# Reciprocals of the softmax denominators on a 128 by 8 tile, with a changed order of visits and four seeds on VectorE

## What is computed

```python
xn = _layernorm(x)
qkv = (xn @ W_qkv).reshape(b, s, 16, 64, 3)
q, k, v = qkv[..., 0], qkv[..., 1], qkv[..., 2]
weights = softmax(einsum('bqhd,bkhd->bhqk', q, k) / 8)
s = einsum('bhqk,bkhd->bqhd', weights, v).reshape(b, s, 1024) @ W_out
x = x + s * silu(mixture_of_experts(xn))
```

## Time and profile before

| | |
|---|---|
| median of 3 runs | 1840.99 us (1839.34 to 1845.72) |
| profiled execution, its own time | 1841.47 us |
| its span, first to last instruction | 1839.6 us |
| mean granted TensorE clock | 0.982 |
| busy: PE, DVE, ACT, POOL | 94%, 84%, 79%, 79% of the span |
| one pair in the middle of the loop | 42.1 us |

### The profile page before, as it was taken

One profiled execution on the slowest core, in us unless ns is written; L12 is line 12 of the kernel. 1 busy time (PEld: TensorE's weight loads), 2 busy tenths in 40 slices (PEclk: granted clock), 3 DMA queues, 4 the chain that ended last, 5 costly groups with the idle time before them and its releaser, 6 DMA issues. The chain is left out here.

```text
span 1839.6 us, 32373 instructions
## 1 busy us (share of the span) xinstructions
PE 1727.4 (94%) x9247; PEld 924.8 (50%) x9247; DVE 1547.9 (84%) x2180; ACT 1459.2 (79%) x1954; POOL 1444.4 (79%) x869
## 2 busy tenths in 40 slices
PE   5899999999999999999999999999999899975687
PEld 5444444444444444444444444444444677763456
DVE  7888888888888888888888888888888878888886
ACT  4488888888888888888888888888888777864553
POOL 5388888888888888888888888888888256654664
PEclk9899999999999999999999999999999999997899
DMA  7212121212212121212122121212122777331000
GB/s 258 79 36 80 36 80 46 80 46 69 78 52 86 34 80 36 80 46 80 46 69 82 51 83 34 80 36 80 46 80 62 241 218 218 115 99 48 0 18 29
DMA packets 125334, 143.31 MB, mean 78 GB/s; under 512 B 26737, under 2 KB 106673, under 8 KB 122098
## 3 DMA queue, kind: packets, MB, share of 16 engines
q1 hardware_dynamic: 120306, 132.61, 23.6%
q0 software_dynamic: 4992, 10.27, 1.7%
HBM read 87.20 MB, written 27.64 MB: 62 GB/s over the span
## 5 line engine op out<-in xcount | busy, mean ns | idle before, releaser
L1562 POOL TENSOR_TENSOR psum_k<-psum_k,probs 128x1024 f32<-128x1024 f32 x384 | 929.3, 2420 | 103.9 <-ACT probs L1499 83.8
L1499 ACT ACTIVATE probs<-ps_s 128x1024 f32<-128x1024 f32 x512 | 497.0, 1024 | 149.9 <-PE ps_s L1319 149.9
L1328 PE MATMUL ps_v<-probs,V 128*64 128x512 f32 x2056 | 497.8, 605 | 0.0
L1581 DVE TENSOR_REDUCE mxh<-ps_three 128x2 f32<-128x1024 f32 x264 | 318.5, 1207 | 98.3 <-PE ps_three L1286 98.2
L1483 ACT ACTIVATE ps_s<-peak 128x1024 f32<-128x1024 f32 x224 | 245.1, 1132 | 0.0
L1483 ACT ACTIVATE ps_s<-qkv_raw 128x1024 f32<-128x1024 f32 x224 | 245.0, 1131 | 0.0
L1622 DVE RECIPROCAL e_y_row<-e_y_row 128x128 f32<-128x128 f32 x256 | 241.0, 941 | 0.0
L1328 PEld LDWEIGHTS ps_v<-probs,V 128*64 128x64 f32 x2056 | 124.8, 136 | 228.6 <-issue 209.7
L1319 PE MATMUL ps_s<-e_ew 64*128 64x512 f32 x1536 | 199.0, 391 | 0.0
L1562 POOL TENSOR_TENSOR psum_k<-probs 128x1024 f32<-128x1024 f32 x64 | 152.8, 2388 | 47.2 <-ACT probs L1499 39.4
L854 POOL DMA_INDIRECT results<-e_y_row,e_y_at x92 | 102.6, 1115 | 82.0 <-ACT e_y_row L795 52.8
(11 more groups left out here) (320 smaller groups left out, 3184.4 us busy)
## 6 DMA issues: line engine op xcount, KB each, us to landing
e_ew<-w_split SPq DMA_DIRECT2D x23, 1024.0 KB
qkv_raw<-peaks SPq DMA_DIRECT2D x33, 512.0 KB, 3.9
V<-e_x_raw SPq DMA_DIRECT2D x33, 512.0 KB, 3.6
peak<-peaks SPq DMA_DIRECT2D x32, 512.0 KB, 4.3
xs_hi<-xh SPq DMA_DIRECT2D x16, 512.0 KB, 4.0
xs_lo<-xl SPq DMA_DIRECT2D x16, 512.0 KB, 5.0
rows<-in_blank_d SPq DMA_DIRECT2D x4, 1483.5 KB, 16.9
e_x_raw<-rows SPq DMA_DIRECT2D x23, 258.0 KB
```

Of the source, the lines that this page charges most:

```text
L1328: ins = nc.tensor.matmul(ps_v[rows, :], V[par][:, kt, rows], probs[:, t % RING, x, :], start=kt == 0, stop=kt == KT - 1)
L1499: nc.scalar.activation(probs[:, t % RING, :, :], ps_s[t % 2][:, :, :], ACT.Exp, scale=SCALE).then_inc(p_done, 1)
L1562: nc.gpsimd.tensor_tensor(acc, probs[:, (t - 1) % RING, :, :] if kt == 1 else acc, probs[:, t % RING, :, :], ALU.add).then_inc(add_done, 1)
L1581: nc.vector.tensor_reduce(mxh[:, kh, t, :], max_bank(unit, i)[:, :, :], AX.X, ALU.max).then_inc(m_done, 1)
```

## The change

It replaces the eight reciprocals of 128 x 128 words of a pair by two of 128 x 8. The denominators of a half are equal over the 64 rows of a head, so 2 x 512 of them are distinct. SP copies one row of each head (`den`) to 128 partitions of 8 words (`flatten`, two DMAs within SBUF), DVE inverts `flat_den` into `flat_inv`, SP writes it to a new DRAM tensor `shares` (`inverse_out`) and spreads it again over 64 rows for each head into `rden` (`inverse_back`, two DMAs). `half_pair` puts these five requests around the two of `spread`. The order of the visits changes, DVE writes the seeds of steps 3, 7, 11 and 15, and the experts' low part (`we_lo`) is made in an output visit. Both halves of a pair now have the same DVE order.

```diff
-    BY_V = (3, 13)
+    BY_V = (3, 7, 11, 15)
-    VISIT = [("K1",), ("Q0", "den1"), ("out0",), ("V0",), ("Q1", "den0"), ("out1",), ("V1",), ("K0",)]
+    VISIT = [("Q0", "den1"), ("out0",), ("K1",), ("V0",), ("Q1", "den0"), ("out1",), ("K0",), ("V1",)]
...
+            def spread_back(unit, hf):
                 sp.wait_ge(mx_out, unit * 16 + 16)
                 sp.dma_start(peak[hf][:, :, :].rearrange("p c x -> p (c x)"), g.peaks[hf:hf + 1, :].to_broadcast([P, 2 * CH])).then_inc(peak_in, 16)
+            def flatten(n, hf):
+                sp.wait_ge(xa_done, reads(n, f"den{hf}"))
+                for x in range(2):
+                    sp.dma_start(flat_den[x * DH:(x + 1) * DH, :], den[x * DH:x * DH + 1, :].rearrange("a (c k) -> a c k", c=DH)).then_inc(inv_moved, 16)
+            def inverse_out(k):
+                sp.wait_ge(inv_done, k + 1)
+                sp.dma_start(g.shares[:, :].rearrange("a (c k) -> (a c) k", c=DH), flat_inv[:, :]).then_inc(inv_moved, 16)
+            def inverse_back(k):
+                sp.wait_ge(inv_moved, inv_moved_out(k))
+                for x in range(2):
+                    sp.dma_start(rden[x * DH:(x + 1) * DH, :], g.shares[x:x + 1, :].to_broadcast([DH, CH])).then_inc(inv_moved, 16)
+            def half_pair(n, unit, hf):
+                k = n * 2 + 1 - hf
+                flatten(n, hf)
+                inverse_out(k)
+                spread(unit, hf)
+                inverse_back(k)
+                spread_back(unit, hf)
...
                 sp.dma_start(xs_hi[:, :].bitcast(F32), g.xh[:, batch].bitcast(F32)).then_inc(xs_in, 16)
                 sp.dma_start(xs_lo[:, :].bitcast(F32), g.xl[:, batch].bitcast(F32)).then_inc(xs_in, 16)
-                spread(n * 2 + 1, 1)
+                half_pair(n, n * 2 + 1, 1)
                 expert_part(n)
                 load_part(n + 1)
-                spread(n * 2 + 2, 0)
-                spread(n * 2 + 3, 1)
+                half_pair(n, n * 2 + 2, 0)
+                half_pair(n + 1, n * 2 + 3, 1)
                 expert_part(n + 1)
                 load_part((n + 2) % N)
-                spread(n * 2 + 4, 0)
+                half_pair(n + 1, n * 2 + 4, 0)
...
-            def inverse(n, hf, part):
-                cols = slice(part * P, (part + 1) * P)
-                v.wait_ge(xa_done, reads(n, f"den{hf}"))
-                ins = nc.vector.reciprocal(rden[:, cols], den[:, cols])
-                if part == PARTS - 1:
-                    ins.then_inc(rden_done, 1)
+            def inverse(n, hf):
+                v.wait_ge(inv_moved, flat_moved(n * 2 + 1 - hf))
+                nc.vector.reciprocal(flat_inv[:, :], flat_den[:, :]).then_inc(inv_done, 1)
...
+                def half(hf, late, early, par):
+                    t = KT - KT * hf
+                    step(t)
+                    step(t + 1)
+                    low(n, early, nxt)
+                    seed(n, t + 3)
+                    row_max_upper(n, t + 2)
+                    row_max_lower(n, t + 2)
+                    row_max_shared(n, t + 3)
+                    inverse(n, hf)
+                    if hf:
+                        expert_part(n)
+                    add_out(n, f"out{1 - hf}")
+                    step(t + 4)
+                    step(t + 5)
+                    low(n, late, par)
+                    seed(n, t + 7)
+                    row_max_upper(n, t + 6)
+                    row_max_lower(n, t + 6)
+                    row_max_shared(n, t + 7)
+                    normalise(n, hf)
+                half(1, "K1", "Q0", nxt)
+                half(0, "K0", "Q1", par)
```

More of the change, by code:

```diff
@@ L993, in layer0_attention @@
     EARLY = 4
-    PARTS = 4
     ADDS = KT - 1
@@ L997, in layer0_attention @@
     PRESETS = 3
-    LATE_PRESETS = 5
+    ONES_PRESETS = 4
+    LATE_PRESETS = 6
     HEADS = [slice(x * DH, (x + 1) * DH) for x in range(2)]
@@ L1012, in layer0_attention @@
     warm = sb("warm", [P, 1], F32)
+    flat_den = sb("flat_den", [P, 2 * CH // P], F32)
+    flat_inv = sb("flat_inv", [P, 2 * CH // P], F32)
     x_rows = sb("x_rows", [P, 2, ROW], F32)
@@ L1060, in layer0_attention @@
     xv_done = sem("xv_done")
-    rden_done = sem("rden_done")
+    inv_done = sem("inv_done")
+    inv_moved = sem("inv_moved")
     picked = sem("picked")
@@ L1072, in layer0_attention @@
     picks_done = sem("picks_done")
-    ones_n_done = sem("ones_n_done")
     n_ready = sem("n_ready")
@@ L1142, in upper, with flat_moved, inv_moved_out, inv_moved_back @@
         return n * len(SHARED) + SHARED.index(t // 2) + 1
+    def flat_moved(k):
+        return k * 80 + 32
+    def inv_moved_out(k):
+        return k * 80 + 48
+    def inv_moved_back(k):
+        return k * 80 + 80
     def chunk(name):
@@ L1175, in spread @@
                 sp.dma_start(g.peaks[hf:hf + 1, :].rearrange("a (s q k) -> q (a s) k", s=2, k=4), mx[:, :, :, :].rearrange("p s t x -> p s (t x)")).then_inc(mx_out, 16)
+            def spread_back(unit, hf):
                 sp.wait_ge(mx_out, unit * 16 + 16)
                 sp.dma_start(peak[hf][:, :, :].rearrange("p c x -> p (c x)"), g.peaks[hf:hf + 1, :].to_broadcast([P, 2 * CH])).then_inc(peak_in, 16)
+            def flatten(n, hf):
[16 more added lines that the diff above has]
+                spread_back(unit, hf)
             load_part(0)
             spread(0, 0)
+            spread_back(0, 0)
             sp.wait_ge(xa_done, AHEAD["a"])
@@ L1200, in _ @@
             sp.wait_ge(peak_in, (N * 2 + 1) * 16)
+            sp.wait_ge(inv_moved, inv_moved_back(N * 2 - 1))
             sp.wait_ge(we_in, (N + 1) * 16)
@@ L1225, in bank_free @@
                 else:
-                    pe.wait_ge(xv_done, n * PER["v"] + AHEAD["v"])
+                    pe.wait_ge(xa_done, n * PER["a"] + AHEAD["a"])
             def projection(n, name, b):
@@ L1358, in _ @@
             pe.wait_ge(picks_done, 1)
-            pe.wait_ge(ones_n_done, 1)
+            pe.wait_ge(preset, ONES_PRESETS)
             for k, left in enumerate((g.before, ones_n)):
@@ L1385, in _ @@
                     p = t // 2
-                    b = (n + (2 if p == VISITS - 1 else 1)) // PAIRS % B
+                    b = (n + (2 if VISIT[p][0] == "K0" else 1)) // PAIRS % B
                     unit, i = maximum(t)
@@ L1451, in read @@
                 else:
-                    act.wait_ge(rden_done, n * 2 + (2 if name == "den0" else 1))
                     nc.scalar.activation(den[:, :], ps_x[:, :], ACT.Copy).then_inc(xa_done, 1)
@@ L1502, in _ @@
                     if p not in SHARED:
-                        read(n, VISIT[p][0], par if p == VISITS - 1 else 1 - par)
+                        read(n, VISIT[p][0], par if VISIT[p][0] == "K0" else 1 - par)
                     for k in (t + 1, t + 2):
@@ L1517, in _ @@
                         read(n, name, 1 - par)
-                    if p == 5:
+                    if p == VISITS // 2:
                         stage(n)
@@ L1526, in _ @@
         def _(pool):
-            nc.gpsimd.memset(ones_n[:, :], 1.0).then_inc(ones_n_done, 1)
+            nc.gpsimd.memset(ones_n[:, :], 1.0).then_inc(preset, 1)
             nc.gpsimd.memset(probs[:, 0, :, :], 0.0).then_inc(preset, 1)
@@ L1565, in _ @@
                         scatter(hf)
-                    if t != STEPS - 5:
+                    if t != STEPS - 7:
                         continue
@@ L1632, in normalise @@
                 k = n * 2 + (1 if hf else 2)
-                v.wait_ge(rden_done, k + 1)
+                v.wait_ge(inv_moved, inv_moved_back(k - 1))
                 v.wait_ge(raw_done, k)
@@ L1663, in tiles_of_experts @@
                 v.wait_ge(n_ready, 2)
-                v.wait_ge(ones_n_done, 1)
+                v.wait_ge(preset, ONES_PRESETS)
                 step(nc.vector.tensor_copy(in_tile[:, :, :], ps_n[1].rearrange("p (t e) -> p e t", e=E)))
@@ L1711, in first_max @@
                     row_max(unit, i)
-            v.sem_inc(rden_done, 1)
             v.wait_ge(w_in, 48)
@@ L2469, in program @@
     g.peaks = nc.dram_tensor("peaks", (2, 2 * CH), F32, kind="Internal").ap()
+    g.shares = nc.dram_tensor("shares", (2, CH), F32, kind="Internal").ap()
     g.results = nc.dram_tensor("results", (2 * NT + ROUTED * CH, D), F32, kind="Internal").ap()
```

## The result

The changed kernel takes 1906.7 us (median of 4 runs, 1900.8 to 1920.4) against 1840.2 before: a ratio of 1.0368, interval 1.0322 to 1.0413. It is 3.7% slower; 1858 was forecast, 1820 to 1880 the range. The profiled execution took 1920.4 us, the slowest of the four.

The account below looks back on a forecast made before the run. PE, busy for 94% of the span, was taken as the bound. 1841.5 us, less 22.4 for the order of visits, plus 39.2 for the even pairs' stop, gave 1858 us, 0.9% slower; range 1820 to 1880.

Parts of the forecast that it names:

- What bounds the kernel, and the place of the loss: PE bounds the kernel; the loss falls in K1 of even pairs, behind VectorE's 2.8 us wait for the copy.
- the step of the queue: Even pairs, half 1: the denominators' copy lands after xs_lo, ahead of it on SP, at +12.3, wanted at +9.5.
- the price of the stop: In K1 of even pairs PE loses 2.45 us, 39 us over 16 pairs, bounds 31 and 51.
- rival: Three rivals: copy not held up (faster), chance 0.22; peaks late too, 0.08; nothing gained, nothing lost, 0.10.
- The gain: New order of visits: V visits save 0.93 us, K visits lose 0.25; net -0.7 per pair, -22.4 over 32.
- the prediction's own sign: Check on pair times: the step of the visits is wrong if odd pairs are not near 41.4 us.
- the step of the visits: V visits, following K visits, go free: -0.93 us per pair; K visits lose 0.25, as the sum precedes their reduction.
- "nothing" for VectorE's relief: VectorE's balance of -4.6 us per pair, from reciprocals and seeds, was booked at nothing by itself, PE being the bound.
- A wait misread: V visits before: PE waits for the reduction's lower half, behind the sum into sT; 0.35 + 0.58 us per pair.
- Later steps of that half: Even pairs, half 1: peaks land at +20.5 to +21, seed 8 due at +21.7; no second stall.
- the two terms: The order of visits, -22.4 us, and the even pairs' stop, +39.2 us, added to 1841.5 us.
- The rule on DMA cost: About 2.0 us per DMA beside its bytes: copy there at +10.3, loss about 0.5 us in an even pair.

Follow-up runs that it names:

- delay256: The change with SP's xs loads and V move kept from ahead of the copy, plus a 128 x 256 reciprocal on VectorE in each even pair; 1902 us.
- delay440: The change with SP's xs loads and V move kept from ahead of the copy, plus a 128 x 440 reciprocal on VectorE in each even pair; 1893 us.
- wide: The change's order of visits and seeds, but reciprocals by VectorE on 128 x 512 in four parts, without DMAs for them; 1922.9 us, ratio 1.0457.
- delay256_ef: As delay256, with the experts' low part put ahead of the 128 x 256 reciprocal on VectorE; 1862.3 us.
- experts_first: The change with the experts' low part ahead of VectorE's wait for the copy instead of behind it; 1858.3 us, ratio 1.0125.
- filler3: The change with three zero-tile matmuls on PE in visit 2 of every even pair, ahead of the wait; 1870.5 us, ratio 1.0170.

## Why the prediction was wrong

- **What bounds the kernel, and the place of the loss: right.** K1 of even pairs, behind a wait of VectorE for the copy: 2.53 us (forecast 2.8), the reciprocal at +12.1 (12.3), PE's second product at 798.88 - 783.55 = +15.3 (15.1), the stop 2.44 (2.45). Part of that agreement is luck: the experts' part took 1.32 and not 0.64, and undisturbed PE would be there at +12.9, not +12.65. What ends the stop is then the end of one of GpSimd's additions, a wait that the prediction doesn't have.
- **Why the copy is late: half right.** Not for being behind them in SP's queue, as the step of the queue has it, but for being issued while they move. From another queue it was as late. Whether by the order of completions or by bandwidth stays open.
- **The failed step is the price of the stop.** "PE loses 2.45 us" counted the stop alone. The clock at half speed after it costs 2.71 more, 43 us over 16 pairs: 5.15 us in an even pair, not 2.45. No rival had it. The profile before showed no stop of PE of this length in the loop, which is why I should have asked what one does.
- **The gain: mis-sized.** -0.7 us per pair was booked and -0.33 measured (11 us for 22); by the prediction's own sign (odd pairs near 41.4, measured 41.8) the step of the visits was wrong. The V visits gave 0.8 (0.93 at most forecast), but the K visits took 0.6 and not 0.25: the sum starts not at once but 0.16 us after PE's output projection ends in K0, and 0.1 later still in K1, behind the stretched experts' part (1.43 in an odd pair). And "nothing" for VectorE's relief was wrong in kind: order alone gave 0.07, the short reciprocal 0.2 to 0.25.
- **A wait misread.** In the V visits of the kernel before, PE's second product did not wait for the lower half of the reduction, which ends at 766.04 when the product has begun at 765.50, but for the sum itself, which ends at 765.44. Moving the sum away was right by either reading. In the second V visit about another 0.2 us came from a reciprocal of 0.94 us ahead of the shared reduction, for which the projection waited. The waits from 400 to 1300 us show PE behind the sum twice in each pair:

```profile
PEld ps_three L1286 <- DVE sT L1641: 18.5, 43, 0.5
```

- **Later steps of that half: right.** No wait for the peaks showed before a seed.
- **The sum.** In the profiled execution the sixteen even pairs cost 79 us more (7.3 of them the first, 50.1 for 42.8), the odd ones 16 x 0.33 = 5 less, and the other stages about 5 more: together the 79 of 1920.4 - 1841.5. With the two terms as measured, 1841.5 - 11 + 16 x 5.15 = 1913 us, between the median and the profiled run. The three other runs have a mean granted clock of 0.959 to 0.961 for its 0.953, so in them the clock was probably low in fewer pairs; there is no trace of them.
- **The rule on DMA cost** that I weighed (the Trainium skill, DMA: Bandwidth & Descriptors, Anatomy of one DMA) would have given 0.5 us in even pairs. The two requests of the copy took 3.0 and 3.9 us from issue to landing in the even pair above, and 1.9 and 2.2 in an odd one, so the trace agrees with the 2.0 only where nothing large moves. Going by the trace was right.

## What to carry to other kernels

A small transfer on which an engine waits in its list should not be issued while large ones move; a queue of its own did not help here, moving the large ones did. Where PE is the bound, price a stop at its length plus what the clock loses after it, and try whether the stop can be made shorter. Take the duration of a VectorE instruction with two SBUF inputs from a place where GpSimd adds at the same time, or keep it away from there.

## What the runs showed of the hardware that I had not expected

A stop of PE of 2.8 us brought 1.2 GHz in all 15 such pairs of the change (nearly 7 us of it in 14), in 14 of 16 in delay256 and 11 of 16 in delay440; one of 2.3 us in 5 of 31 in wide, one of 2.0 us in 2 of 16 in delay256_ef, one of 1.7 to 1.8 us in 3 of 15 in experts_first. A filler of matmuls by zero in the stop prevented it in all 16 of filler3. Six zero matmuls of 512 float32 columns take 5.36 us, twice my figure. The experts' part (`we_lo`) takes from 0.55 to 0.67 us in the kernel before and up to 2.60 in wide, by when GpSimd's addition in flight ends; normalisation, with two SBUF inputs as well, went from 1.52 us on average to 2.13 in the change.
